# Expert layers kept in sorted order: a finished tile is routed during later pieces and scattered into a region for each expert

## The reference

```
def _unipool_layer(xt, router, W1, W2):     # xt [2048,128]
    probs = softmax(xt @ router)            # 16 experts
    w, idx = max(probs), argmax(probs)
    for i in range(16):
        h = silu(xt @ W1[i]) @ W2[i]        # 128 -> 512 -> 128
        out += where(idx == i, w, 0) * h
xt = layernorm(x)
for router in routers: xt = _unipool_layer(xt, router, W1, W2)   # 4 layers, one W1 and W2
x = x + xt
```

## Time and profile before

| | |
|---|---|
| three runs, median | 588.83 us (587.71 to 590.13) |
| profiled execution | 590.55 us, span of its instructions 588.8 us |
| mean granted TensorE clock | 0.958 |
| busy: PE, DVE, ACT, POOL | 494.8 (84%), 330.3 (56%), 276.3 (47%), 196.5 us (33%) |
| DMA | 28.11 MB, 48 GB/s over the span |
| last h and y matmuls of layers 0 to 3 start at | 282.7, 377.3, 476.0, 575.2 us |
| indirect DMAs of POOL | 64 gathers (mean 963 ns), 64 scatters (970 ns) |

### The profile page before, as it was taken

The page is one execution under the profiler, slowest core; times in us unless marked ns, Lnnn a source line. Parts: engine busy times, 40 slices in busy tenths (PEclk is TensorE's granted clock), DMA queues, the critical chain, the costliest instruction groups (busy, mean ns, idle before and its releaser), DMA issues.

```text
span 588.8 us, 16874 instructions
## 1 busy us (share of the span) xinstructions
PE 494.8 (84%) x5788; PEld 404.1 (69%) x5788; DVE 330.3 (56%) x746; ACT 276.3 (47%) x684; POOL 196.5 (33%) x243
## 2 busy tenths in 40 slices
PE   2599999979878759999867999967899986799794
PEld 1377777767645328999434999733799953599792
DVE  2468777866758693455285455348355427554352
ACT  1277776775762415665103666311466510266450
POOL 8222333221030144325325415504432531541342
PEclk9989999998998898999998999997899999799998
DMA  5100000295000201001301100120110130110005
GB/s 139 30 22 21 21 13 20 90 351 157 3 2 2 71 13 36 26 19 38 91 1 36 32 8 37 46 67 13 32 30 14 41 91 1 32 32 12 24 37 156
DMA packets 30690, 28.11 MB, mean 48 GB/s; under 512 B 4624, under 2 KB 24464, under 8 KB 30608
## 3 DMA queue, kind: packets, MB, share of 16 engines
q1 hardware_dynamic: 26512, 18.62, 10.8%
q0 software_dynamic: 4096, 8.40, 4.5%
HBM read 20.71 MB, written 6.29 MB: 46 GB/s over the span
## 4 chain that ended last, share of the span: by engine, by line
PE 61%; DVE 15%; issue 7%; DMA 6%; ACT 4%; POOL 4%; another core or an unknown queue 1%; SPq 1%; DVEq 0%; POOLq 0%; ACTq 0%
PE bank L794 19%; PE bank L807 18%; PE bank L636 6%; PE bank L617 5%; DMA cur<-token_rows 3%; PE bank L595 3%; DVE ohr L1084 2%; DVE ppT L911 2%; DMA ppT<-token_rows,token_i 2%; DMA token_rows<-ysort,token_i 2%; PE bank L589 1%; PE bank L783 1%; POOL token_rows L390 1%; PE bank L576 1%
## 5 line engine op out<-in xcount | busy, mean ns | idle before, releaser
L1133 DVE SCALAR_TENSOR_TENSOR pp<-pp,bank 128x512 f32<-128x512 f32 x124 | 85.3, 688 | 129.6 <-ACT pp L532 124.0
L807 PE MATMUL bank<-w,pp 128*128 x992 | 137.4, 282 | 14.1 <-DVE pp L1133 12.4
L794 PE MATMUL bank<-vm,ppT 128*128 x992 | 136.1, 281 | 0.1
L807 PEld LDWEIGHTS bank<-w,pp 128*128 128x128 f32 x992 | 123.1, 195 | 17.3 <-issue 16.7
L794 PEld LDWEIGHTS bank<-vm,ppT 128*128 128x128 f32 x992 | 124.2, 197 | 1.7 <-issue 0.4
L532 ACT ACTIVATE pp<-bank 128x512 f32<-128x512 f32 x124 | 74.1, 598 | 100.7 <-PE bank L794 88.2
L523 ACT COPY ppT<-w 128x512 f32 x124 | 75.9, 612 | 60.2 <-DVE piece_tile L1106 59.7
L390 POOL DMA_INDIRECT token_rows<-ysort,token_i x64 | 62.1, 970 | 106.8 <-DVE ysort L1143 92.0
L383 POOL DMA_INDIRECT ppT<-token_rows,token_i x64 | 61.6, 963 | 66.3 <-PE bank L783 38.7
L690 PE MATMUL bank<-trib,onesb 128*128 128x512 bf16 x308 | 76.8, 407 | 0.0
L447 ACT ACTIVATE pp<-bank,nmax 128x128 f32<-128x128 f32 x256 | 67.8, 423 | 0.0
(11 more groups left out here) (182 smaller groups left out, 527.3 us busy)
## 6 DMA issues: line engine op xcount, KB each, us to landing
w<-in_L_ffn_W_dram SPq DMA_DIRECT2D x1, 4096.0 KB, 14.7
cur<-token_rows SPq DMA_DIRECT2D x16, 256.0 KB, 3.9
cx<-in_ctx_dram SPq DMA_DIRECT2D x16, 128.0 KB, 2.2
token_rows<-cur SPq DMA_DIRECT2D x1, 1024.0 KB, 5.1
ppT<-token_rows,token_i POOLq DMA_INDIRECT x64
token_rows<-ysort,token_i POOLq DMA_INDIRECT x64
out_dram<-xs SPq DMA_DIRECT2D x4, 256.0 KB, 2.8
xs<-in_x_dram SPq DMA_DIRECT2D x1, 768.0 KB, 6.2
```

The lines of the kernel that those rows point to most:

```text
L794: last = mm(banks[2 + j % 2][:, c * P:(c + 1) * P], w1_piece[:, j % 2, c * P:(c + 1) * P], xT[:, ds(tile_of[j] * P, P)], start=True, stop= ...
L807: last = mm(banks[6 + j % 2][:, 0:D], hh[:, j % 2, c * P:(c + 1) * P], w2[:, ds(e * FF + c * P, P)], start=(c == 0), stop=(c == FC - 1))
L1133: v.scalar_tensor_tensor(hh[:, j % 2, :], th[:, j % 2, :], 1.0, banks[2 + j % 2][:, :], ALU.add, ALU.mult).then_inc(s["h_ready"], 1)
```

## The change

All layers are written out (no hardware loop). The rows stay in sorted order from layer to layer, and what the inversion was needed for travels with a row: a row is 132 floats wide, 128 channels and behind them OLD (column 128), GATE (129) and ID (130).

- DRAM holds `expert_rows`, 2048 rows for each of 16 experts. A row is scattered to (expert x 2048 + its rank in the expert), and the next layer gathers its 16 tiles by `source_i`, which DVE computes from the experts' counts (`sources`). ACT clears this region with 16 DMAs during attention (`clear_region`), one a tile.
- The tiles of a layer are routed in parts (`PARTS`: tiles 0-3, 4-7, 8-10, 11-13, 14-15), each when its last piece is added: PE transposes the finished tile (`transpose_y`), ACT copies it (`evac_yT`), PE computes its logits (`logits_y`), DVE and ACT compute the choice (`largest`, `exponentials`, `choose`, `weigh`), PE the ranks (`ranks`), DVE the places (`put`), and POOL scatters the part. In steps 18 to 32 this stands between pieces; parts 3 and 4 come behind the last piece.
- y is kept without its gate (`wpiece` is a one-hot now). The gate goes along in the row; logits of y are multiplied by it within the exponential and `largest`. The next layer multiplies each gathered tile by the gate in OLD (`scale`) ahead of the transpose. Layer 0 gathers the layer norm, which needs no gate.
- x2 is stored as rows; at the end POOL gathers them by ID in sorted order, DVE adds gate times y (`finish`), and POOL scatters tiles straight into the output.
- Layer 0 is routed in quarters, and its 16 tiles are scattered too, before the first gather.
- W1 and W2 are loaded in 32 DMAs between the context loads, and not in two.

```diff
+            def scatter_rows(r):
+                for b, (a, z) in enumerate(parts(r)):
+                    pool.wait_ge(s["place_ready"], nth_part(r, b))
+                    for t in range(a, z):
+                        g.indirect_dma_start(out=region, out_offset=...place_i[:, t:t + 1]...,
+                            in_=yrows[(r + 1) % 2][:, t, :], in_offset=None).then_inc(s["scattered"], 16)
+            def gather_rows(layer):
+                for t in range(NT):
+                    if t == 0:
+                        pool.wait_ge(s["source_ready"], 2 * layer + 1)
+                        pool.wait_ge(s["scattered"], (layer + 1) * 16 * NT)
...
@@ tensor: step(i) @@
-                        pe.wait_ge(gathered[i % 4], layer * OF_FOUR + (i // 4 + 1) * 16)
+                        if layer == 0:
+                            pe.wait_ge(gathered[i], 16)
+                        else:
+                            pe.wait_ge(s["scaled"], (layer - 1) * NT + i + 1)
...
+                    if routes and 0 <= i - 18 < NT - 1:
+                        transpose_y(i - 18)
+                    if routes and 0 <= i - 19 < NT - 2:
+                        logits_y(i - 19)
...
+                    if routes:
+                        for b in ending(i - 21):
+                            ranks(r, b)
...
-                stay_warm(banks[5], 28)
+                if routes:
+                    logits_y(NT - 2)
+                    transpose_y(NT - 1)
+                    stay_warm(banks[7], 2)
+                    logits_y(NT - 1)
+                    ranks(r, 3)
+                    stay_warm(banks[7], 6)
+                    ranks(r, 4)
+                    stay_warm(banks[7], 34)
@@ vector @@
+            def scale(layer, t):
+                dve.wait_ge(gathered[t], (layer + 1) * 16)
+                v.tensor_scalar(xin[:, t, 0:D], xin[:, t, 0:D], xin[:, t, OLD:OLD + 1], None, ALU.mult) \
+                    .then_inc(s["scaled"], 1)
...
                 def step(i):
+                    if layer > 0 and 2 <= i < NT:
+                        scale(layer, i)
                     if 0 <= i - 1 < PIECES:
                         j = i - 1
                         dve.wait_ge(s["tanh_done"], count(j + 1))
...
-                        sorted_tile = ysort[:, ds(tile_of, 1), :].rearrange("p a d -> p (a d)")
+                        sorted_tile = yrows[layer % 2][:, ds(tile_of, 1), 0:D].rearrange("p a d -> p (a d)")
...
+                    if routes:
+                        for b in ending(i - 19):
+                            largest(r, b)
+                        for b in ending(i - 20):
+                            choose(r, b)
+                            weigh(r, b)
+                        for b in ending(i - 22):
+                            put(r, b)
+                    elif 0 <= i - 17 < NT:
+                        finish(i - 17)
...
+                if routes:
+                    choose(r, 3)
+                    weigh(r, 3)
+                    largest(r, 4)
+                    put(r, 3)
+                    choose(r, 4)
+                    weigh(r, 4)
+                    put(r, 4)
```

More of the change, by code:

```diff
@@ L163, in perceiver_block @@
         scored = [sem(f"scored{r}") for r in range(4)]
[L164 to L167, removed]
+        gathered = [sem(f"gathered{t}") for t in range(NT)]
+        x2_gathered = [sem(f"x2_gathered{t}") for t in range(NT)]
+        rowsT_evac = [sem(f"rowsT_evac{q}") for q in range(4)]
         attention_weights = [
@@ L185, in each_tile, with parts, nth_part, logits_bank @@
                 body(t, t % 2, first=t == 0, last=t == NT - 1)
[L187 to L191, removed]
+        def parts(r):
+            return QUARTERS if r == 0 else PARTS
+        def nth_part(r, b):
+            return b + 1 + (0 if r == 0 else len(QUARTERS) + (r - 1) * len(PARTS))
+        def logits_bank(r, b):
+            return banks[(4, 6)[b % 2] if r == 0 else (1, 4)[b % 2]]
+        def experts(a, z):
+            return slice(a * E, z * E)
+        def ending(tile):
+            return [b for b, (a, z) in enumerate(PARTS) if z - 1 == tile]
         def piece_steps(step):
@@ L401, in _ @@
+            pool.wait_ge(s["region_cleared"], 16 * E)
+            scatter_rows(0)
+            for layer in range(L):
+                gather_rows(layer)
+                if layer + 1 < L:
+                    carry_ids(layer)
+                    scatter_rows(layer + 1)
+                else:
+                    finish_rows()
         @block.scalar
@@ L481, in _ @@
             std_of(3, slice(0, NT))
[L482 removed]
+            normalise_odd_quarters(0, cur)
             evac_tiles()
@@ L696, in transpose_tiles @@
                     for k in range(4):
-                        last = nc.tensor.transpose(banks[q][:, k * P:(k + 1) * P], cur[:, 4 * q + k, :],
+                        last = nc.tensor.transpose(banks[q][:, k * P:(k + 1) * P], tiles[:, 4 * q + k, 0:D],
                                                    ident[:])
@@ new lines, in blocks, with ranks, count_in @@
+            def blocks(a, z):
+                return banks[5][:, a * E:z * E]
+            def ranks(r, b):
+                a, z = parts(r)[b]
+                top = z + 1 if z == NT else z
+                def count_in(first, hot, start=False, stop=False):
+                    return mm(blocks(first, top).rearrange("p (k e) -> p k e", e=E), onesb[:],
+                              hot.unsqueeze(1).broadcast_to([P, top - first, E]), start=start, stop=stop)
+                if b >= 1:
+                    pe.wait_ge(s["place_ready"], nth_part(r, b - 1))
+                count_in(a, region_part[:], start=True)
+                for k in range(a):
+                    count_in(a, ohb[:, experts(k, k + 1)])
+                pe.wait_ge(s["oh_ready"], nth_part(r, b))
+                for k in range(a, z):
+                    hot = ohb[:, experts(k, k + 1)]
+                    if k + 1 < top:
+                        count_in(k + 1, hot)
+                    last = mm(blocks(k, k + 1), trib[:], hot, start=False, stop=(k == z - 1))
+                last.then_inc(s["rank_done"], 1)
```

474 lines of the change are left out of this document (250 added, 224 removed).

## The result

| | kernel before | changed kernel |
|---|---|---|
| median (lowest to highest) | 589.48 us (587.71 to 590.32, 4 runs) | 705.25 us (701.39 to 710.19, 4 runs) |
| ratio, 95% interval | | 1.197 (1.189 to 1.206) |
| profiled execution, its span | 590.55, 588.8 | 701.39, 699.6 |
| first h to last y, layers 0 to 3 | 62.2, 62.0, 64.9, 66.7 | 84.9, 102.5, 100.9, 107.2 |
| last y to the next first h | 32.6, 33.8, 32.5 | 20.1, 19.4, 21.6 |

The changed kernel is 20% slower. Forecast were 627 us and at most 655. The direction was right and the size wrong: 116 us more, where 38 were forecast.

The account below looks back on a forecast made before the run. PE was taken to bound the layers, with a chain through DVE, POOL and DMA between them. Terms -45.4 + 10.5 - 9.7 + 27 + 56 = +38.4 on 590.55 gave 629, or 627 us at the median; range 606 to 655.

Parts of the forecast that it names:

- Early pieces, a new loop: Layers 1 to 3, tiles 2 to 15: DVE's rescale behind the accumulation closes a loop, 1.36 us a step; +56 us.
- The pauses, and POOL's issuing put at nothing: Layers: the pause at a layer's start might vanish, 3 us less a layer; POOL's 48 DMAs, 60 us, fit in a layer.
- The clock: Inside the loop: granted clock left at 1.00, 2.4 GHz, as in the gap of the earlier profile.
- the rival of the half clock: In the loop the clock falls to half: +0.9 us a step, +38, 665 us, or 646 for half the steps; chance 0.15.
- Late pieces: Steps 18 to 32 of layers 0 to 2: routing work on PE, DVE and ACT adds 9 us a layer; +27 us.
- Layer ends: Three gaps between layers: first h 17.8 us after the last y, POOL's scatters being late; -45.4 us.
- T0: The time of a layer's last y, from which the gap to the next first h is counted.
- The start of layer 0: Before layer 0: 16 scatters must land before the gathers, first h at 230.8 instead of 220.3; +10.5 us.
- The end: After the last y: one add and one scatter replace landing, reload, add and store, 3.8 us for 13.5; -9.7 us.
- Elsewhere: Attention and POOL's waits: ACT's 16 clearing DMAs and POOL's extra work cost nothing, or 6 us if cover is gone.

Follow-up runs that it names:

- a1_scale_ahead: Changed kernel with DVE rescaling each gathered tile two steps earlier in its stream; 654.51 us, ratio 1.112.
- a2: Changed kernel with POOL's gathers, those of x2 too, waiting for PE's progress instead of going back to back; 661.04 us, ratio 1.121.
- a3: Changed kernel with both edits, the rescale two steps earlier and the gathers paced by PE; 602.49 us, ratio 1.022.
- a8: a6 with a POOL memset of 512 columns behind each of the scatters of tiles 8 to 13; ratio 1.001.
- a7: a6 with the four scatters of each of the first two parts spaced one per piece; ratio 0.998.
- b2_sp: Kernel before with 10 plain loads of 128 rows a layer added, issued back to back by SP; 588.75 us, ratio 1.001.
- b1_burst: Kernel before with 10 more back-to-back indirect gathers on POOL in mid-layer, into unused memory, in each layer; 643.59 us, ratio 1.094.
- b5_narrow: b1_burst with its 10 added gathers moving rows of 16 bytes in place of 512; 646.80 us, ratio 1.093.
- a6: a3 without the x2 gathers: SP stores x2 into the output and the last layer's scatters add to it; 593.71 us, ratio 1.004.
- a9: a6 with SP and not POOL waiting for the landing of the last 16 scatters; ratio 0.999.
- b3_spaced: b1_burst with a POOL memset of 512 columns behind each of its 10 added gathers; 601.31 us, ratio 1.023.

## Why the prediction was wrong

By its own steps, against the changed kernel unless said otherwise:

- **Early pieces, a new loop, +56: right.** 3.22 us a step for 3.2 to 3.4, and 51 us for the place of the rescale (a1_scale_ahead), 59 where no pause hides part of it (a2 less a3). The transpose waits 0.9 us for the rescale, where 1.3 was forecast.
- **The pauses, and POOL's issuing put at nothing: the step that failed.** I took the pause of the earlier trace rows for a fixed 3 us that might vanish, and POOL, being off the chain of waits, for free ("48 DMAs of 1.26 us are 60 us of a layer that lasts longer than that"). The change takes POOL's waits away, and its 16 gathers in a row make the pause 12 us in each layer, and its x2 gathers add one of 15.7 us in layer 3. Pacing them gave back 44 us, though a2 itself has a burst at its end that costs 15. That is more than half of the 78 us by which the forecast was short. In the layers, 139.6 us were added where 27 and 56 were forecast, 57 too few; the gains of 44 and 15 together are of that size.
- **The clock.** I left it alone, and in the loop by itself it is 1.00 (a2, 341 to 380). In the changed kernel it was at half for 31 us in layer 1 (335.9 to 366.6). That stretch began ahead of the first h, behind 5 us in which TensorE had waited, as in a2 (329.1 to 339.3); but here it lasted through the pause, and steps behind it take up to 4.7 us for 3.2. So the rival of the half clock was in part right in the trace and wrong in its cause. The Trainium skill (TensorE: Matmul & The Clock Gate, section HAM oscillation — how this bites in real kernels) has a loop whose waits are longer than its bursts of matmuls and that starts every burst at the half clock. The prediction set this against the loop here as a rival; the waits in it are 0.9 us of each 3.2, and they did not bring the half clock; around the pauses of 12 us the trace agrees: in layer 1 of a1_scale_ahead the clock is at half from 346.1 to 359.7, and the tanh of the pause are at 341.10 and 353.90.
- **Late pieces, +27: right.** For steps of 2.2 us there are four of 2.3 to 2.5 and behind them uneven ones of 1.3 to 3.5; in layer 1 of a3 the last 16 steps take 38.3 us, before 28.6: 9.7 a layer for 9.
- **Layer ends, -45.4: 7.7 too good.** 20.1, 19.4 and 21.6 us from T0 to the first h, not 17.8. Of the 2.3 us more in the first gap POOL idles 2.17 for the places of the last part, which are late by the 4.3 us of DVE's wait above: the same cause again (a8).
- **The start of layer 0, +10.5: right.** First h at 232.39, forecast 230.8.
- **The end, -9.7: 6.8 too good.** It was -2.9. The 3.8 us forecast have no term for what stands behind POOL's last wait, a drain of 6.45 us. The kernel before has one of 4.55 us, but there it starts at 579.36 and lies beside the last loads and adds. Taking work off the other engines left it bare.
- **Elsewhere, 0: right.** The 17.3 MB of clearing cost attention nothing that shows: 119.8 us of busy TensorE from 30 to 160, before 119.3, and the first h of layer 0 came within 1.6 us of its forecast.

In the layers the half clock around the pauses and the short bursts of four scatters have their part as well; I have not separated them (a7 shows the latter to be small). Why POOL's issuing holds PE up is open: whether the array stands still or only its increments are late. In layer 1 two increments 0.1 us apart speak for the latter, in layer 0 a y that signals 2.2 us after the h before it for the former. The Trainium skill (SBUF — State Buffer, section Who interferes with whom) says that "DMA never contends with a compute engine". For SP's loads b2_sp agrees; with indirect DMAs from POOL TensorE's results come late, which costs 55 us in b1_burst and 54 in b5_narrow, whether or not one calls that contention.

No version here beats the kernel before. a6, a7, a8 and a9 stand level with it (1.004, 0.998, 1.001, 0.999): the gaps give up to 38 us, the routing in the late pieces (29 us) and the start of layer 0 (12 us) take them back, and POOL's drain keeps the end from giving more than 3.

## What to carry to other kernels

Count the indirect DMAs that an edit lets POOL issue in a row. An engine off the chain of waits is not free when its instructions disturb the one that bounds the kernel, and a wait that looks like a nuisance (four buffers for sixteen tiles) can be what keeps it harmless. Where a semaphore wait ends long after the producer's record, look at what every other engine does in that stretch, and then copy that work alone into a quiet place, as b1_burst did. An operation put into an in-order stream costs by its place: the same rescale cost 51 us behind the accumulation and nothing two steps earlier.

## What the runs showed of the hardware

- Indirect DMAs in a row, 1.25 us apart, make tanh start late behind the recorded end of its h: runs of 15 and 16 by 5.5 to 13 us (15.6 at the end of a3); the 10 of b1_burst with the gather ahead of them by 10.8 to 11.6; the seven of the kernel before by 2.0 to 3.5; four by 1.9 to 3.4. With 1.65 us between their starts (b3_spaced) it is 1.5 us at most. Rows of 16 and of 512 bytes do the same.
- How far into the run the delay sets in differs: in layer 1 of the changed kernel the tanh is on time when nine gathers have started, in layer 0 it is 1.8 us late after seven.
- POOL's closing drain is longer in the kernels with more indirect DMAs: 4.55 us with 128, 5.14 with 144, 6.45 with 160, 8.63 with 168. That the number is the reason is not shown.
- An indirect scatter that adds holds POOL for 1.55 us, a plain one 0.96 (a6, a9).
- An indirect gather of 128 rows holds POOL for 946 ns with 16 bytes a row, as with 512 (b5, b1).
